# A transposed block of softmax shifts: one transpose of 48 columns and four transfers in place of four transposes of 12 columns and one transfer

## The reference, cut to what matters

```python
def _L0_attn_ref(x, Wq, Wk, Wv, Wo, bo):
    ...
    s = jnp.einsum('bqhd,bkhd->bhqk', q * scale, k)
    causal = jnp.tril(jnp.ones((t, t), dtype=bool))
    s = jnp.where(causal[None, None], s, -jnp.inf)
    p = jax.nn.softmax(s, axis=-1)
    o = jnp.einsum('bhqk,bkhd->bqhd', p, v).reshape(b, t, H * HD)
    return o @ Wo + bo
...
x = L0_attn_x
x = x + _L0_attn_ref(_layernorm(x, axis=-1), ...)
x = x + _L0_ffn_ref(_layernorm(x, axis=-1), ...)
```

## Time and profile before

| | |
|---|---|
| median of 3 runs | 506.52 us (505.99 to 507.28) |
| span of the profiled execution | 527.7 us |
| TensorE matmuls busy | 469.7 us, 4121 instructions |
| VectorE busy | 413.1 us |
| ScalarE busy | 358.9 us |
| GpSimd busy | 286.6 us |
| mean of the DMA traffic | 104 GB/s |

### The profile page before, as it was taken

One profiled execution on the slowest core, in us unless ns is written; L12 is line 12 of the kernel. 1 busy time (PEld: TensorE's weight loads), 2 busy tenths in 40 slices (PEclk: granted clock), 3 DMA queues, 4 the chain that ended last, 5 costly groups with the idle time before them and its releaser, 6 DMA issues.

```text
span 527.7 us, 14330 instructions
## 1 busy us (share of the span) xinstructions
PE 469.7 (89%) x4121; PEld 328.0 (62%) x4121; DVE 413.1 (78%) x1519; ACT 358.9 (68%) x782; POOL 286.6 (54%) x579
## 2 busy tenths in 40 slices
PE   3788999999999999999999999989788789999981
PEld 1545656556555545546555545459688679999980
DVE  6898878988988888888888897875556555557875
ACT  7576877777867867876866857875456457777750
POOL 5603544535755766657657565725456555545542
PEclk9879999999999999999999999999999899999997
DMA  7434232132233233233333326722222322235653
GB/s 225 134 93 129 56 118 91 56 118 88 67 120 108 70 108 110 76 101 97 102 95 98 106 76 175 209 65 63 56 63 69 85 77 74 71 79 180 182 172 101
DMA packets 49454, 54.92 MB, mean 104 GB/s; under 512 B 6564, under 2 KB 41554, under 8 KB 49377
## 3 DMA queue, kind: packets, MB, share of 16 engines
q1 hardware_dynamic: 44736, 45.18, 29.5%
q0 software_dynamic: 4320, 8.47, 4.7%
q10 hardware_dynamic: 320, 0.36, 0.2%
HBM read 34.96 MB, written 17.90 MB: 100 GB/s over the span
## 4 chain that ended last, share of the span: by engine, by line
PE 50%; DVE 28%; ACT 7%; issue 7%; DMA 4%; another core or an unknown queue 3%; ACTq 1%; SPq 0%; POOL 0%; DVEq 0%; POOLq 0%
PE psO L1035 12%; DVE psS L1349 10%; PE psT L1197 7%; DVE maxs L1352 7%; PE psS L998 7%; PE psM L1208 5%; PE psO L1208 5%; PE psT L1011 3%; PE psS L1197 2%; ACT PT L811 2%; DMA xs_t<-sorted_x 2%; PE psS L1187 2%; DVE maxs L1349 1%; DVE xn L1278 1%
## 5 line engine op out<-in xcount | busy, mean ns | idle before, releaser
L811 ACT ACTIVATE PT<-psT 128x512 f32<-128x512 f32 x320 | 172.5, 594 | 67.6 <-PE psO L1035 45.0
L1349 DVE CUSTOM_DVE_ANT_0 psS<-mask_row,psS 128x512 f32<-128x512 bf16 (+1 forms) x232 | 142.8, 624 | 33.6 <-PE psS L998 29.3
L998 PE MATMUL psS<-Ks,Qs 96*128 96x128 bf16 (+3 forms) x512 | 132.9, 308 | 9.5 <-DVE maxs L1352 7.3
L598 POOL TENSOR_SCALAR_AFFINE_SELECT PT<-PT 128x512 f32<-128x512 f32 x124 | 76.8, 635 | 96.0 <-ACT PT L811 94.8
L1011 PE MATMUL psT<-Qs,Ks 108*128 108x384 bf16 (+3 forms) x512 | 109.9, 299 | 4.2 <-ACT PT L811 3.0
L695 POOL DMA_INDIRECT token_y<-Qs,y_row x71 | 70.8, 997 | 74.6 <-DVE Qs L1750 39.0
L998 PEld LDWEIGHTS psS<-Ks,Qs 96*128 96x128 bf16 x512 | 50.4, 99 | 53.5 <-DVE maxs L1352 26.4
L629 POOL DMA_INDIRECT sorted_x<-xn,place x64 | 64.3, 1005 | 27.6 <-issue 16.5
L1352 DVE TENSOR_REDUCE maxs<-psS 128x2 f32<-128x512 f32 (+3 forms) x120 | 75.7, 669 | 1.8 <-PE psS L1001 1.4
L1035 PE MATMUL psO<-PT,Vs 128*32 128x512 f32 (+3 forms) x1024 | 75.8, 436 | 0.3 <-DVE x_all L1375 0.3
L1011 PEld LDWEIGHTS psT<-Qs,Ks 108*128 108x128 bf16 x512 | 43.5, 97 | 32.8 <-ACT PT L811 12.9
(11 more groups left out here) (260 smaller groups left out, 741.1 us busy)
## 6 DMA issues: line engine op xcount, KB each, us to landing
Qs<-q_parts SPq DMA_DIRECT2D x96, 96.0 KB
Ks<-k_parts SPq DMA_DIRECT2D x95, 96.0 KB
xs_t<-sorted_x SPq DMA_DIRECT2D x71, 65.0 KB
w_sb<-in_L_ffn_w SPq DMA_DIRECT2D x16, 256.0 KB
k_parts<-kparts SPq DMA_DIRECT2D x8, 384.0 KB, 2.6
q_parts<-qparts SPq DMA_DIRECT2D x8, 384.0 KB, 3.6
x_all<-in_L_attn_x SPq DMA_DIRECT2D x8, 256.0 KB, 4.7
v_all<-token_y SPq DMA_DIRECT2D x4, 512.0 KB, 4.4
```

The source lines that it names most:

```text
L598: pool.affine_select(out=square, in_=square, compare_op=ALU.is_ge, fill=0.0, base=0, pattern=[[0, GH], [1, P]], channel_multiplier=-1).the ...
L811: act.activation(PT[:, n * T:(n + 1) * T], psT[:, bank, :], ACT.Exp).then_inc(prob_done[bank], 1)
L998: last = pe.matmul(psS[:, bank, c0:c0 + n], Qs[0:QK_ROWS, g, h, j * P:n], Ks[0:QK_ROWS, g, h, 0:n], start=True, stop=alone)
L1349: dve.tensor_tensor_reduce(src, mask_row[:, (CH - 1 - j) * P:], src, 1.0, NEG, ALU.add, ALU.max, maxs[:, par, j, h:h + 1]).then_inc(scores ...
```

## The change

What a step's shift rows are doesn't change, nor which engine does which part. `mparts` holds for each query 48 numbers, block by part by head. Before, each block's 12 columns are turned by a transpose of their own, into 128 columns each of `psM`, so the result is 12 rows of 512. Now all 48 columns are turned by one transpose, and the result is 48 rows of 128, where rows 12j to 12j+11 belong to block j. ScalarE copies 48 rows of 128 in place of 12 rows of 512. The rows of a block lie on different partitions then, and four transfers, each of 12 rows of 128 numbers times 4 heads, put them beside one another in `Qs`. The semaphore `shift_loaded` rises by 64 a step in place of 16, and its waits count so. The bytes written to `Qs` are the same 48 KB, in pieces of 256 bytes in place of 1024.

```diff
-        shiftT = sb("shiftT", [SHIFTS, 2, T], BF16)
+        shiftT = sb("shiftT", [CH * SHIFTS, 2, P], BF16)
...
+        SHIFT_LOADS = CH * 16
...
             def load_shift(s, g):
                 sp.wait_ge(shiftT_copied, s + 1)
-                sp.dma_start(Qs[SHIFT0:SHIFT0 + SHIFTS, g, :, :],
-                             shiftT[:, g % 2, :].unsqueeze(1).to_broadcast([SHIFTS, GH, T])).then_inc(shift_loaded[g], 16)
+                for j in range(CH):
+                    sp.dma_start(Qs[SHIFT0:SHIFT0 + SHIFTS, g, :, j * P:(j + 1) * P],
+                                 shiftT[j * SHIFTS:(j + 1) * SHIFTS, g % 2, :].unsqueeze(1).to_broadcast([SHIFTS, GH, P]))\
+                        .then_inc(shift_loaded[g], 16)
...
-                    act.wait_ge(shift_loaded[(g + 2) % GROUPS], (b + 1) * 16)
-                act.activation(shiftT[:, g % 2, :], psM[0:SHIFTS, 0:T // 2].bitcast(BF16), ACT.Copy)\
+                    act.wait_ge(shift_loaded[(g + 2) % GROUPS], (b + 1) * SHIFT_LOADS)
+                act.activation(shiftT[:, g % 2, :], psM[0:CH * SHIFTS, 0:P // 2].bitcast(BF16), ACT.Copy)\
                     .then_inc(shiftT_copied, 1)
...
-                    pe.wait_ge(shift_loaded[g], (b + 1) * 16)
+                    pe.wait_ge(shift_loaded[g], (b + 1) * SHIFT_LOADS)
...
             def turn_shift(s, b, g):
                 pe.wait_ge(shift_split[g % 2], b * 2 + g // 2 + 1)
-                for j in range(CH):
-                    last = pe.transpose(psM[0:SHIFTS, j * P // 2:(j + 1) * P // 2].bitcast(BF16),
-                                        mparts[:, g % 2, j, :, :].rearrange("p i h -> p (i h)"), identb[:, :])
-                last.then_inc(shiftT_ready, 1)
+                pe.transpose(psM[0:CH * SHIFTS, 0:P // 2].bitcast(BF16),
+                             mparts[:, g % 2, :, :, :].rearrange("p j i h -> p (j i h)"), identb[:, :]).then_inc(shiftT_ready, 1)
```

## The result

| | before | changed |
|---|---|---|
| median of 4 runs | 506.9 us (505.99 to 507.62) | 512.82 us (512.43 to 515.75) |
| ratio, 95% interval | | 1.0125 (1.0096 to 1.0154) |
| span of the profiled execution | 527.7 us | 510.7 us |

The changed kernel is 1.25% slower, about 6 us; a repetition later gave 1.0134 (1.0098 to 1.017). The forecast was 506.5, with a range to 512.0, so the result lies above the range. The profiled execution of the changed kernel ran in 512.43 us, so 1.7 us lie around its span.

A forecast was written before the change was run, and what follows sets the result against it. The prediction took TensorE and VectorE, in turns with the transposes between weighing and first new scores, to bound the kernel. A 4.2 us gain against 4.15 us of late landings gave -0.05, so 506.5 us, range 503.7 to 512.0.

The forecast's parts named there:

- The path: Within a step TensorE and VectorE take turns; VectorE idles 1.3 us for the first new scores, with the transposes before them.
- The transposes: Three of four fewer on TensorE each step, wider load free: 0.17 us in each of 25 steps, 4.2 us gained.
- The copy: ScalarE's copy of the shift rows takes about 270 ns, 0.30 us less; counted only as SyncE's head start.
- The transfers: Four on SyncE take 4.7 us from first issue to last landing (4.5 to 5.07), hidden in ordinary steps with 0.67 to spare.
- Prologue: Before the first step TensorE already waits for the landing; issue 0.47 us earlier, landing 2.1 later: 1.65 us lost.
- The step at 292.46: SyncE issues late here, straight from its loads, so the copy's head start is worth nothing: 0.8 us lost.
- The step at 329.50: The landing comes 0.5 us late, less about 0.3 for which the second matmul waits anyway: 0.2 us lost.
- The last step: Shift rows land at 342.27 against a use at 340.76, with the weighing behind it on TensorE: 1.5 us lost.
- SyncE's queue: k loads and stores of k behind the transfers wait 3.3 and 3.0 us anyway, so the additional 2.5 us fit; experts' loads stay hidden.
- queue: Theory written for the experiments: the transfers' 2.5 us on SyncE's queue, or small packets, delay other traffic in every step.
- the transposes are worth nothing: Rival: VectorE starts earlier but is held elsewhere, so only the 4.15 us of losses remain: 510.7 us; chance 0.12.
- Late in every step: Rival: `probs` task 0 waits for `shift_loaded` in ordinary steps, about 28 steps late by some 0.2 us: 515 us; late landing's chance 0.24.

The follow-up runs named there:

- halves_1_30: Kernel before with two transposes of 24 columns and two transfers in steps 1 to 30, old form in 0 and 31: 504.9 against 507.07 us, ratio 0.9952.
- scores_first: Kernel before with score task 3 moved ahead of the four transposes: 508.55 against 506.82 us, ratio 1.0028.
- four_transfers: Kernel before, four transposes and wide copy kept, with the one transfer split into four in all steps: 515.05 against 506.74 us, ratio 1.0163.
- middle_new: Kernel before with the changed form in steps 1 to 25 only: 510.07 against 506.74 us, ratio 1.0054.
- last_new: Kernel before with the changed form in step 31 alone: 509.82 against 506.74 us, ratio 1.0056; run again, ratio 1.0038.
- halves_middle: Kernel before with two transposes of 24 columns and two transfers in steps 1 to 25: 505.25 against 506.82 us, ratio 0.998.
- last_warm: last_new with eight unused matmuls before TensorE's wait for the landing in step 31: 508.15 us against the kernel before's 507.07, ratio 1.0016.

## Why the prediction was wrong, point by point

- **The path** was read rightly in its result, that the transposes cost step time: halves_1_30 gains 0.095 us a step by two fewer. The reason given, that VectorE waits for the first new scores, is not all of it: scores_first brings these scores 0.2 us earlier and loses, so TensorE's own work counts too.
- **The transposes, -4.2 us.** This is the first step that failed, in the sentence "a load is hidden behind the matmul before it; I take no charge". A load of 12 columns is, one of 48 isn't behind this weighing: 0.113 us later start (309 - 196 ns) in 25 steps, 20 of them in steps 2 to 25, which is 2.3 of the 4.1 us that were counted there. The 0.17 us was nearly right for what it is: 319 - 169 = 150 ns less between first transpose and scores. The wider load was the one part without a bound of its own: the rows show loads of 12 columns alone, and an extra 0.1 us in 25 steps would have put the sum at +2.5 us.
- **The copy.** 258 ns, predicted 270. That it is worth nothing but a head start was wrong: it moved GpSimd's mask onto VectorE's `xn`, +0.38 us in four steps, 1.5 us. The 20 other steps from 2 to 25 gain 1.6 us together, 0.08 each; the sum is the measured -0.1. That the two nearly cancel is the chance of this kernel's timing.
- **The transfers.** First issue to last landing is 4.54 us in the prologue's chain (4.7 taken, bounds 4.5 and 5.07), issue 0.80 each. The price was right where nothing disturbs. Four transfers don't take the estimated 8 us of four times the 2.0 that the Trainium skill gives for GpSimd's path (DMA: Bandwidth & Descriptors, Anatomy of one DMA). The Trainium skill's advice to coalesce small transfers (DMA: Bandwidth & Descriptors, Rules for kernel authors) holds here: four_transfers loses 8.3 us by the split alone. What the bounds missed is the spread: I took one undisturbed landing for all steps. From first issue to a use that waited it is 5.9 us in the changed kernel's step 15, 5.3 in steps 28 and 31, and over 6 twice in middle_new.
- **Prologue, 1.65 us.** The distance from transposes to use grew by 1.57, and the stage by 1.2 us at a like clock. In the table it grew by 3.0, since the partner profile has no half clock there and the changed kernel's has 6.9 us; that varies with the old form too.
- **The step at 292.46, 0.8 us.** +1.0.
- **The step at 329.50, 0.2 us.** -0.1 (8.50 to 8.42), although TensorE waited 0.25 us there for shift rows; it fits with a wait that was there anyway. Step 28, which the prediction took as hidden, waited 0.4 and 0.6 us in the two profiles.
- **The last step, 1.5 us.** The second step that failed, +4.3. Its lateness was 2.1 us by the use, in place of 1.5, as the landing took longer than in the prologue; at full clock some 1.7 of it remain in the stage, and 1.1 with the landing of last_new. The larger error is in the sentence on TensorE's granted clock, "it is taken as unchanged": TensorE stood still for 2.5 us and then worked 6.8 us at half speed, on the weighing and what follows it, which cost 2.5 to 2.65 us by the table of the last step.
- **SyncE's queue.** Right: the k loads and the stores still wait for their releasers, and nothing else was late in the changed kernel's two profiles. The *queue* theory, as a cost in every step, fell with four_transfers, where 22 of 24 middle steps kept their length, and halves_1_30 with 30 more transfers is faster. As a cost now and then it isn't excluded: in halves_middle a load of q parts was 1.25 us late, and whether the additional transfers had a part in it is not shown.
- **The rivals.** None as written. Closest is "the transposes are worth nothing", 510.7 us, for another reason than the one it gave; its sum left the clock out. "Late in every step" did not happen, but single steps are late now and then.

The sum as it should have been: middle -0.1, prologue 1.2, step 26 1.0, last step 1.7 at full clock, that is 3.8 us, and 2.6 of half clock in the last step, 6.4. Measured 5.9 and 6.6. The fit is partly luck. The sum has nothing for the clock in the prologue. And the -0.1 comes from two profiles, while middle_new, over 12 runs, lost 3.3 us with the changed form in steps 1 to 25 alone. How much of the 2.6 the average execution pays stays open too: the mean clocks are as low in the other runs of the changed kernel, but last_warm's time could not tell it apart. Half clock comes behind other waits as well: halves_middle's profile has 3.4 us of it at 293 us, in step 26 with the old form, and that step took 11.77 us in place of 9.18. There TensorE had waited for q parts:

```profile
292.86 1.01 PE L1029 MATMUL psS<-Ks,Qs 96*128 96x512 bf16 x2 [1.25 <-DMA Qs<-q_parts]
```

## What to carry to other kernels

A merged instruction is not only fewer instructions: check on the trace whether its weight load still starts ahead of the matmuls before it, since a wider one may have to wait for them to end. Price a wait of some us on TensorE by the work behind it at half the clock too, and look at the granted clock after each wait that a change adds, above all where a stage begins or ends. And where a merge costs transfers, merge halfway and only where there is slack: two transposes and two transfers in steps 1 to 30 gained 2.2 us where the full merge lost 6.

## What the runs showed of the hardware

- Behind matmuls whose weights are 128x32, a transpose with 12 or 24 columns of weights starts 196 ns after the start of the last of them, with 36 or 48 (or scores with 128) 309 ns or a little more.
- Four transfers of 12 KB from SBUF to SBUF, issued 0.82 to 0.92 us apart, landed 1.96 us after the last issue began; one of 48 KB landed after 2.56. In two steps of another kernel's execution four took 6.2 and 6.5 us from first issue to use.
- A wait of 1.8 us on TensorE was followed by full clock in one execution and by 3.4 us at 1.2 GHz in another of the same kernel. The work behind it took 9.2 us at full clock and 10.5 with the 3.4 us at half. Waits of 2.5 to 2.7 us at the same place were followed by 6.8 us at half clock in three of three profiles.
- A tensor_scalar on VectorE of 0.34 us took 0.75 beside a mask on GpSimd that began with it, and 0.34 where the mask began 0.2 us later.
